# The first feed-forward's preparation moved into the attention ahead of it

## The chip, the cores and the metric

The kernel runs on one core of one Trainium2 chip. The time is device microseconds of one execution. The engines of a core are TensorE (matrix products and transposes through the array, into PSUM), VectorE, ScalarE, GpSimd, and SyncE, which here only issues loads. They run side by side and wait for each other through semaphores.

## The reference

A decoder block with gated cross-attention, four levels deep, over x of 4 batches of 1024 rows of 256. Every level adds a gated attention and a gated feed-forward:

```
x = x + tanh(g_xattn[0]) * attention_0(layernorm(x), ctx)
x = x + tanh(g_ffn[0])   * ffn_0(layernorm(x))
...                                    # three more levels
```

Attention 0 is a two-way cross-attention between x and 77 context rows with a sigmoid gate. Feed-forward 0 is a "bit linear" layer, a depthwise convolution over three neighbouring rows, SiLU, and a second bit linear layer:

```
def act_quant(x):                      # per row
    scale = 127.0 / clip(max(abs(x), axis=-1), 1e-05)
    return clip(round(x * scale), -128, 127) / scale
def weight_quant(w):                   # per matrix
    scale = 1.0 / clip(mean(abs(w)), 1e-05)
    return clip(round(w * scale), -1, 1) / scale
h = act_quant(x) @ weight_quant(w1).T  # 256 -> 1024
h = silu(depthwise_conv1d(h, conv_w, conv_b))
y = act_quant(h) @ weight_quant(w2).T  # 1024 -> 256
```

The mean of all of |w1| and of all of |w2| must be known before a weight can be rounded, and the maximum of a row before the row can be.

## The kernel before

All of x stays in SBUF, as 32 tiles of 128 rows by 256 (`sh.x`). The program is a row of eight stages, one function each. A stage opens a scope of its own for its tiles and semaphores; at its end all engines meet at a barrier and the semaphores are cleared. So nothing of a stage runs beside the stage before it.

**Stage 1, `stage_l0_xattn`** (attention 0). SyncE's queue loads the context, the weights and x batch by batch; ScalarE's queue loads biases, small weights and, last, the rows and the bands. The loop `for b in range(B)` runs over the 4 batches and is skewed: `out`, `gate` and `update` of batch b-1, in four quarters, stand between the steps of batch b. In order of time, for one batch, the names are these.

- VectorE `norm` makes the normalised rows. TensorE `front` transposes them (L915), ScalarE `turned` copies them (L679), and TensorE makes the scores in both directions (L878).
- VectorE `scores` (L758 to L769) takes maxima, ScalarE `exps` (L684, L689) the exponentials, VectorE `sums` (L776 to L779) the sums.
- TensorE transposes (L978), ScalarE copies them out (L706, `p2t`), and TensorE mixes the rows into the context (L989, into bank `ub`, "the mixing"). VectorE `mixed` (L783) scales the outcome.
- TensorE `out` (L967, L968), ScalarE `gate` (L697), VectorE `update` (L799 to L803, then the statistics of two tiles, L209), once for each quarter.

VectorE's order in batch b is `scores(b)`, `update(b-1, 0)`, `sums(b)`, `mixed(b)`, in batch 1 a norm chain over 16 tiles, `update(b-1, 1)`, `norm`, `update(b-1, 2)`, `norm`, `update(b-1, 3)`. The four updates of the last batch come behind the loop. `norm_range` is the norm chain: 19 small steps that turn statistics into a scale and a shift for each tile.

**Stage 2, `stage_l0_ffn`** (feed-forward 0). SyncE loads w1 and w2 (1 MB each) and two small arrays (`cw`, `cb`). Ahead of the loop over slots stands a chain: ScalarE sums |w1| and |w2| (L466, L468), TensorE adds the sums over the partitions (L371), VectorE makes the scales (L300 to L304). ScalarE loads the SiLU table (L472) and normalises tiles 0 to 7 (L479). VectorE takes their maxima (L283) and the scales, and rounds w1 in three passes (L307 to L309). ScalarE quantises the tiles (L486), VectorE takes the added constant off (L297), TensorE transposes them in four pairs through one bank (L380), and ScalarE copies each pair out (L493). Then comes ScalarE's scaling of w2 (L530), and the first up-projection (L390). A slot `g` is one batch and one of 8 blocks of 128 hidden rows: up-projection (L390), ScalarE's centre tap (L501), VectorE's two outer taps (L319, L321), ScalarE's SiLU (L507). The second layer follows 9 slots behind.

Of the kernel before, what the change touches and what calls it, by code (L numbers as in the profile page):

```python
# [16 lines left out]
P = 128  # L17
# [195 lines left out]
def stage_l0_ffn(nc, io, sh):  # L213
# [3 lines left out]
    s = scope(nc, "l0f")  # L217
    HID = 4 * D
# [7 lines left out]
    with s.ctx:  # L226
        norm_sems(s)
        w1, w2 = s.sb("w1", [P, DC, HID]), s.sb("w2", [P, M, D])
        w2q = s.sb("w2q", [P, M, D], BF16)
        wsum, wscale, wmean = s.sb("wsum", [P, 2]), s.sb("wscale", [P, 2]), s.sb("wmean", [P, 2])  # L230
        cw, cb = s.sb("cw", [P, M, 3]), s.sb("cb", [P, M])
        xn = s.sb("xn", [P, TB, D])
        am, sc, inv1 = (s.sb(n, [P, TB]) for n in ("am", "sc", "inv1"))
# [11 lines left out]
        for n in ["w_loaded", "small_loaded", "wsum_ready", "wtot_ps", "wscale_ready", "w1_ready", "w2_scaled", "w2_ready", "table_loaded",  # L245
                  "rstd_ready", "norm_ready", "step", "insc_ready", "q1_ready", "xd_ready", "xt_ps", "xt_ready", "h_ps", "a_ready",
                  "conv_ready", "z_ready", "am2_step", "sc2_ready", "inv2_ready", "zt_ps", "zq_ready", "back_ps", "q2_ready", "y_ps",
                  "x_ready", "stats_ready"]:
            s[n] = s.sem(n)
# [17 lines left out]
        with nc.Block() as block:  # L267
            @block.sync
            def _(sp):
                sp.dma_start(w1[:, :, :], io.L0_ffn_w1_T.rearrange("(c p) o -> p c o", p=P)).then_inc(s.w_loaded, 16)  # L270
                sp.dma_start(w2[:, :, :], io.L0_ffn_w2_T.rearrange("(c p) o -> p c o", p=P)).then_inc(s.w_loaded, 16)
# [4 lines left out]
            def _(dve):  # L276
                c = norm_vector(nc, dve, sh, s)
                dve.sem_inc(s.rstd_ready, 1)
                k = Chain(dve, s.step)

                def largest_input(b, j, n):
                    dve.wait_ge(s.norm_ready, b * TB + j + n)
                    k.link(nc.vector.tensor_reduce(am[:, j:j + n], xn[:, j:j + n, :], AX.X, ALU.max, apply_absolute_value=True))  # L283

                def input_scales(b):
                    k.link(nc.vector.tensor_scalar(am[:, :], am[:, :], 1e-5, None, ALU.max))
                    if b:
                        dve.wait_ge(s.xd_ready, b * TB)
# [3 lines left out]
                    dve.wait_ge(s.insc_ready, b + 1)  # L292
# [6 lines left out]
                dve.wait_ge(s.wtot_ps, 1)  # L299
                c.link(nc.vector.tensor_scalar(wmean[:, :], yb[:, 0:2], 1.0 / (HID * D), 1e-5, ALU.mult, ALU.max))  # L300
                nc.vector.reciprocal(wscale[:, :], wmean[:, :]).then_inc(s.wscale_ready, 1)
                dve.wait_ge(s.wscale_ready, 1)
                c.link(nc.vector.tensor_scalar(wmean[:, 0:1], wmean[:, 0:1], 1.0 / 127.0, None, ALU.mult))
                c.link(nc.vector.tensor_scalar(wmean[:, 1:2], wmean[:, 1:2], tg, None, ALU.mult))  # L304
# [64 lines left out]
            def _(pe):  # L369
                pe.wait_ge(s.wsum_ready, 2)  # L370
                nc.tensor.matmul(yb[:, 0:2], sh.ones[:, :], wsum[:, :], start=True, stop=True).then_inc(s.wtot_ps, 1)  # L371

# [50 lines left out]
                def down(t):  # L423
                    if t == 0:
                        pe.wait_ge(s.w2_ready, 1)
                        pe.wait_ge(s.wscale_ready, 1)
# [12 lines left out]
                pe.wait_ge(s.w1_ready, 1)  # L439
# [24 lines left out]
            def _(act):  # L464
                act.wait_ge(s.w_loaded, 32)
                nc.scalar.activation(z[:, 0:2, :], w1[:, :, :].rearrange("p m d -> p (m d)").rearrange("p (a b) -> p a b", a=2), ACT.Abs,  # L466
# [2639 lines left out]
```

## Time and profile before

| | us |
|---|---|
| median of three runs | 1948.39 (1948.32 to 1948.67) |
| the profiled execution's own time | 1948.08 |
| span of its profile | 1946.1 |
| TensorE / VectorE / ScalarE / GpSimd busy | 1656.8 / 1148.0 / 886.7 / 321.2 |

The profile is one execution. A row of a timeline gives the start, the busy time, the engine, the source line, the operation, the tile written and the tiles read, the shapes, and the number of instructions taken together; in square brackets stands the idle time of the engine ahead of it and what ended it. PE is TensorE, DVE VectorE, ACT ScalarE. Times are in us from the start of the span. The granted clock is TensorE's, as a share of full speed.

### The profile page before, as it was taken

The numbers are of one execution on the slowest core, as the hardware profiler recorded it, in microseconds if no ns is written. First come the engines' busy times: TensorE is split into PE (matmuls) and PEld (weight loads), VectorE is DVE, ScalarE is ACT, GpSimd is POOL, SyncE is SP. The second block draws the span as 40 slices with busy tenths as digits, with TensorE's granted clock in tenths as the row PEclk, the third lists the DMA queues.
The fourth block names the chain that finished last, engine by engine and source line by source line (L and its number), as shares of the span: only waits on it lengthen the run. The fifth ranks groups of instructions, "written<-read, shape, count | busy, mean of one in ns | idle before, by whom it ended". The sixth has DMA issues, their size and how long they took to land. (4 is left out here: it accounts for less than half of the span.)

```text
span 1946.1 us, 29978 instructions
## 1 busy us (share of the span) xinstructions
PE 1656.8 (85%) x10149; PEld 1254.6 (64%) x10149; DVE 1148.0 (59%) x2495; ACT 886.7 (46%) x1803; POOL 321.2 (17%) x359
## 2 busy tenths in 40 slices
PE   7895578896899997899997579999954999979998
PEld 5452245555677665588886269999944888854446
DVE  4765567676455556899887743322247889842115
ACT  2232567764443210365564345555544566533213
POOL 0000000000000001311100155555553111101110
PEclk9898799998899988999998779999977999979999
DMA  5001000002100000100001922222252000010002
GB/s 154 1 1 44 0 1 1 1 1 68 49 1 1 1 1 9 30 1 1 2 2 55 382 82 72 72 72 72 72 168 67 2 1 2 1 47 1 1 0 87
DMA packets 62845, 78.78 MB, mean 40 GB/s; under 512 B 13179, under 2 KB 52655, under 8 KB 62319
## 3 DMA queue, kind: packets, MB, share of 16 engines
q1 hardware_dynamic: 42967, 47.35, 7.4%
q0 software_dynamic: 7584, 20.72, 3.4%
q10 hardware_dynamic: 12152, 8.85, 1.5%
q8 instruction: 84, 1.38, 0.3%
q14 instruction: 58, 0.48, 0.1%
HBM read 58.16 MB, written 18.74 MB: 40 GB/s over the span
## 5 line engine op out<-in xcount | busy, mean ns | idle before, releaser
L2880 PEld LDWEIGHTS moe_bank<-moe_xt,moe_w1e 128*128 128x128 f32 x1264 | 155.0, 193 | 5.7 <-DVE moe_xt L2728 1.7
L2880 PE MATMUL moe_bank<-moe_xt,moe_w1e 128*128 128x128 f32 x1264 | 155.8, 277 | 1.1 <-DVE moe_xt L2728 1.1
L2890 PE MATMUL moe_bank<-moe_w,moe_xin 128*128 x632 | 149.3, 379 | 0.0
L2954 ACT ACTIVATE moe_xin<-moe_bank,moe_b 128x128 f32<-128x128 f32 x316 | 90.1, 368 | 125.8 <-PE moe_bank L2880 124.2
L390 PE MATMUL l0f_hb<-l0f_xt,l0f_w 128*128 128x512 f32 x256 | 126.0, 624 | 5.4 <-DVE l0f_a L321 3.8
L1092 POOL TENSOR_TENSOR all_x<-all_x,l1f_bias 128x256 f32 x32 | 23.1, 724 | 632.2 <-DVE l1f_xn L204 632.2
L2890 PEld LDWEIGHTS moe_bank<-moe_w,moe_xin 128*128 128x128 f32 x632 | 114.0, 190 | 12.3
L209 DVE BATCH_NORM_STATS2 all_stats<-all_x 128x6 f32<-128x256 f32 (+1 forms) x256 | 104.0, 422 | 8.4
L2737 DVE TENSOR_TENSOR moe_y<-moe_bank,moe_b2r 128x256 f32<-128x256 f32 x79 | 33.6, 425 | 119.0 <-PE moe_bank L2890 116.1
L2797 POOL DMA_INDIRECT moe_results<-moe_y,moe_row x79 | 78.0, 987 | 125.1 <-DVE moe_y L2737 121.1
L2728 DVE COPY moe_xt<-moe_bank 128x256 f32<-128x256 f32 x79 | 33.6, 425 | 106.2 <-PE moe_bank L2868 105.1
L1964 PE MATMUL l3f_bank<-l3f_xt,l3f_wx 128*128 128x512 f32 x192 | 88.1, 609 | 0.0
L2945 ACT ACTIVATE moe_w1e<-moe_w 128x1024 f32 x79 | 83.5, 1058 | 2.9 <-issue 1.9
L2404 PE MATMUL l3x_o_bank<-l3x_vrow,l3x_pt 128*128 128x136 f32 (+1 forms) x640 | 81.2, 282 | 0.0
L2792 POOL DMA_INDIRECT moe_xin<-moe_inputs,moe_token x79 | 76.8, 972 | 26.3 <-PE moe_bank L2868 21.0
L2404 PE MATMUL l2x_o_bank<-l2x_vrow,l2x_pt 128*128 128x136 f32 (+1 forms) x640 | 80.7, 281 | 0.0
L390 PEld LDWEIGHTS l0f_hb<-l0f_xt,l0f_w 128*128 128x128 f32 x256 | 47.0, 200 | 48.7 <-issue 47.8
L2404 PEld LDWEIGHTS l3x_o_bank<-l3x_vrow,l3x_pt 128*128 128x128 f32 (+1 forms) x640 | 77.1, 191 | 0.5
L319 DVE SCALAR_TENSOR_TENSOR l0f_a<-l0f_hb,l0f_cw,l0f_a 128x1023 f32<-128x1023 f32 x32 | 41.0, 1282 | 61.5 <-ACT l0f_a L501 61.5
L2404 PEld LDWEIGHTS l2x_o_bank<-l2x_vrow,l2x_pt 128*128 128x128 f32 (+1 forms) x640 | 76.4, 190 | 0.6
L2042 ACT ACTIVATE l3f_gate<-l3f_bank,l3f_cols 128x512 f32<-128x512 f32 x36 | 24.7, 687 | 105.4 <-PE l3f_bank L1972 105.4
L1886 DVE TENSOR_TENSOR l3f_prod<-l3f_gate,l3f_ct 128x512 f32<-128x512 f32 x12 | 8.3, 692 | 94.1 <-ACT l3f_gate L2042 94.1
(478 smaller groups left out, 3812.1 us busy)
## 6 DMA issues: line engine op xcount, KB each, us to landing
moe_w<-in_L_ffn_W SPq DMA_DIRECT2D x32, 512.0 KB, 10.3
moe_w<-moe_results SPq DMA_DIRECT2D x16, 512.0 KB, 8.8
all_x<-in_x SPq DMA_DIRECT2D x4, 1024.0 KB, 13.1
out_x<-all_x SPq DMA_DIRECT2D x8, 512.0 KB, 2.9
l0f_w<-in_L_ffn_w_T SPq DMA_DIRECT2D x2, 1024.0 KB, 6.4
moe_inputs<-moe_xin ACTq DMA_DIRECT2D x8, 256.0 KB, 7.3
moe_inputs<-moe_w1e ACTq DMA_DIRECT2D x8, 256.0 KB, 7.5
moe_b2r<-in_L_ffn_b SPq DMA_DIRECT2D x1, 2048.0 KB, 14.0
```

What stands on the lines that cost most here:

```text
L209: return nc.vector.bn_stats(sh.stats[:, ds(t * 6, 6)], x_tile(sh, t))
L319: k.link(nc.vector.scalar_tensor_tensor(a[:, u, 1:S], h[:, 0:S - 1], cw[:, m, 0:1], a[:, u, 1:S], ALU.mult, ALU.add))
L390: ins = nc.tensor.matmul(hb[g % 2][:, half * 512:(half + 1) * 512], w1[:, d, m * P:(m + 1) * P], xt[:, b % 2, d, half * 512:(half + 1) * 5 ...
L1964: ins = nc.tensor.matmul(bank[3 * m + k][:, :], wx[:, k, c, m * P:(m + 1) * P], xt[:, c, b * S + j * G:b * S + (j + 1) * G], start=(c == 0 ...
L2404: ins = nc.tensor.matmul(o_bank[:, m * VW:(m + 1) * VW], pt[0:rows(i), u, n, j * P:(j + 1) * P], vrow[0:rows(i), ds((t // TB) * (DC * NV * ...
L2728: nc.vector.tensor_copy(xt[:, u, :], bank[3 * u][:, 0:D]).then_inc(s.et_ready, 1)
L2792: nc.gpsimd.indirect_dma_start(out=gathered(t), out_offset=None, in_=xnd, in_offset=bass.IndirectOffsetOnAxis(ap=token[:, t:t + 1], axis=0 ...
L2797: nc.gpsimd.indirect_dma_start(out=ys, out_offset=bass.IndirectOffsetOnAxis(ap=row[:, t:t + 1], axis=0), in_=y[:, u, :], in_offset=None).t ...
L2880: ins = nc.tensor.matmul(out, w1e[:, at:at + P], xt[:, u, c * P:(c + 1) * P], start=(c == 0), stop=(c == DC - 1))
L2890: ins = nc.tensor.matmul(bank[4 + u][:, 0:D], ht[:, u, c * P:(c + 1) * P], w2[:, ds(e * (HC * D) + c * D, D)], start=(c == 0), stop=(c == ...
L2945: nc.scalar.activation(w1e[:, u * DC * HID:(u + 1) * DC * HID], w1[:, ds(e * (DC * HID), DC * HID)], ACT.Copy).then_inc(s.w1e_ready, 1)
L2954: ins = nc.scalar.activation(ht[:, u, m * P:(m + 1) * P], bank[1 + u][:, m * P:(m + 1) * P], ACT.Gelu, bias=b1[:, ds(e * HC + m, 1)])
```

## The change

The weights of feed-forward 0, their sums, scales and the rounding of w1, and the normalised rows of batch 0 with their maxima and scales are made in stage 1. Their tiles get a scope `sh.f0` around both stages. Both loads go to the end of SyncE's queue in stage 1. ScalarE's two Abs instructions stand at the end of the loop body of `b == 0`, behind `exps(1)`; they write to `w2q` in place of `z`. TensorE's sum over the partitions goes to the end of batch 1, ahead of `front(2)`, into bank `ub`. VectorE gets `weight_scales` (scales and the first pass over w1) at the end of batch 1, `round_weights` (the other two passes) at the end of batch 2, and in batch 3 `norm_range` over tiles 0 to 7 ahead of `update(2, 2)`, `next_inputs` (eight `normalise` steps, on VectorE now) ahead of `update(2, 3)`, and `next_scales` behind it. Stage 2 begins with the quantise steps. Its norm chain covers tiles 8 to 31 and stands behind the dequantise steps, and the SiLU table is loaded behind the four copies. The rounding of w2 stays where it was.

```diff
 # stage 2
-                sp.dma_start(w1[:, :, :], io.L0_ffn_w1_T.rearrange("(c p) o -> p c o", p=P)).then_inc(s.w_loaded, 16)
-                sp.dma_start(w2[:, :, :], io.L0_ffn_w2_T.rearrange("(c p) o -> p c o", p=P)).then_inc(s.w_loaded, 16)
...
-                c = norm_vector(nc, dve, sh, s)
-                dve.sem_inc(s.rstd_ready, 1)
+                c = Chain(dve, s.norm_step)
...
-                largest_input(0, 0, TB)
-                input_scales(0)
-                c.link(nc.vector.tensor_scalar(w1[:, :, :], w1[:, :, :], wscale[:, 0:1], MAGIC, ALU.mult, ALU.add))
-                c.link(nc.vector.tensor_scalar(w1[:, :, :], w1[:, :, :], MAGIC, 1.0, ALU.subtract, ALU.min))
-                nc.vector.tensor_scalar(w1[:, :, :], w1[:, :, :], -1.0, None, ALU.max).then_inc(s.w1_ready, 1)
                 for t in range(TB):
                     dequantise(t)
+                norm_range(nc, c, sh, TB, T)
+                dve.sem_inc(s.rstd_ready, 1)
...
                 for t in range(TB):
-                    norm(t)
-                for t in range(TB):
                     quantise_x(t)
                 for t in range(0, TB, 2):
                     copy_x(t)
-                act.wait_ge(s.wscale_ready, 1)
+                act.wait_ge(s.small_loaded, 32)
+                nc.scalar.activation(silu_in[:, :], cb[:, :], ACT.Silu).then_inc(s.table_loaded, 1)
+                act.wait_ge(s.table_loaded, 1)
 # stage 1: SyncE, ScalarE, VectorE, TensorE
+                sp.dma_start(f.w1[:, :, :], io.L0_ffn_w1_T.rearrange("(c p) o -> p c o", p=P)).then_inc(sh.f0_loaded, 16)
+                sp.dma_start(f.w2[:, :, :], io.L0_ffn_w2_T.rearrange("(c p) o -> p c o", p=P)).then_inc(sh.f0_loaded, 16)
...
                     if b + 1 < B:
                         turned(b + 1)
                         exps(b + 1)
+                    if b == 0:
+                        act.wait_ge(sh.f0_loaded, 32)
+                        nc.scalar.activation(f.w2q[:, :, :].rearrange("p m d -> p (m d)"), f.w1[:, :, :].rearrange("p m d -> p (m d)"), ACT.Abs,
+                                             accum_out=f.wsum[:, 0:1]).then_inc(sh.f0_wsum, 1)
+                        act.wait_ge(sh.f0_wsum, 1)
+                        nc.scalar.activation(f.w2q[:, :, :].rearrange("p m d -> p (m d)"), f.w2[:, :, :].rearrange("p m d -> p (m d)"), ACT.Abs,
+                                             accum_out=f.wsum[:, 1:2]).then_inc(sh.f0_wsum, 1)
...
                     if b + 1 < B:
                         norm(b + 1, 0, NP)
+                    else:
+                        dve.wait_ge(s.xn_ready, T)
+                        dve.wait_ge(s.stats_ready, 2 * TB)
+                        norm_range(nc, c, sh, 0, TB)
                     if b:
                         update(b - 1, 2)
                     if b + 1 < B:
                         norm(b + 1, NP, TB)
+                    else:
+                        next_inputs()
                     if b:
                         update(b - 1, 3)
+                        if b == 1:
+                            weight_scales()
+                        elif b == 2:
+                            round_weights()
+                        else:
+                            next_scales()
...
+                    if b == 1:
+                        pe.wait_ge(sh.f0_wsum, 2)
+                        pe.wait_ge(s.shared_set, 1)
+                        nc.tensor.matmul(ub[:, 0:2], sh.ones[:, :], f.wsum[:, :], start=True, stop=True).then_inc(sh.f0_wtot, 1)
                     if b + 1 < B:
                         front(b + 1)
```

## Rows read from the trace of the kernel before

**Rows 1.** The page: the span, and each engine's busy time.

```profile
span 1946.1 us, 29978 instructions
PE 1656.8 (85%) x10149; PEld 1254.6 (64%) x10149; DVE 1148.0 (59%) x2495; ACT 886.7 (46%) x1803; POOL 321.2 (17%) x359
```

**Rows 2.** Busy time by stretch: its length, engines (instructions), granted clock, DMA share, GB/s.

```profile
179.30:213.58 34.28, 5.01 (x18) 3.38 (x19) 13.01 (x39) 15.25 (x27) 0.00 (x0) 0.51 0.20 62
213.58:1946.10 1732.52, 1503.45 (x9507) 1161.37 (x9507) 1026.86 (x2176) 821.65 (x1672) 312.29 (x342) 0.94 0.12 40
```

**Rows 3.** Timeline of ScalarE, start of stage 2.

```profile
188.89 1.91 ACT L466 ACTIVATE l0f_z<-l0f_w 128x2048 f32<-128x2048 f32 x1 [13.05 <-DMA l0f_w<-in_L_ffn_w_T]
...
192.81 1.28 ACT L472 ACT_TABLE_LOAD   x1
...
194.34 4.04 ACT L479 ACTIVATE l0f_xn<-all_x,all_shift,all_rstd 128x256 f32<-128x256 f32 x8
201.60 3.30 ACT L486 ACTIVATE l0f_xn<-l0f_xn,l0f_sc 128x256 f32<-128x256 f32 x8 [3.22 <-DVE l0f_sc L291]
207.26 0.60 ACT L493 ACTIVATE l0f_xt<-l0f_back 128x512 f32<-128x512 f32 x1 [2.36 <-PE l0f_back L380]
...
219.18 1.20 ACT L501 ACTIVATE l0f_a<-l0f_hb,l0f_cb,l0f_cw 128x1024 f32<-128x1024 f32 x1 [2.87 <-PE l0f_hb L390]
```

**Rows 4.** Timeline of VectorE, start of stage 2.

```profile
180.67 0.21 DVE L168 TENSOR_TENSOR all_var<-all_stats 128x32 f32<-128x32 f32 x1 [1.38 <-PEq L107]
...
198.49 2.29 DVE L283 TENSOR_REDUCE l0f_am<-l0f_xn 128x8 f32<-128x2048 f32 x1 [4.22 <-ACT l0f_xn L479]
...
201.60 1.29 DVE L307 TENSOR_SCALAR l0f_w<-l0f_w,l0f_wscale 128x2048 f32<-128x2048 f32 x1
```

**Rows 5.** Timeline of TensorE, start of stage 2 (the second row holds two slots).

```profile
206.08 1.08 PE L380 MATMUL l0f_back<-all_ident,l0f_xn 128*128 128x128 f32 x4 [12.65 <-DVE l0f_xn L297]
...
213.58 8.99 PE L390 MATMUL l0f_hb<-l0f_xt,l0f_w 128*128 128x512 f32 x16 [0.84 <-ACT l0f_xt L493]
```

**Rows 6.** Busy time by stretch, early in stage 1 (columns as in rows 2).

```profile
28.00:30.00 2.00, 2.00 (x3) 0.50 (x2) 0.00 (x0) 0.00 (x0) 0.00 (x0) 0.50 0.03 8
```

**Rows 7.** Timeline of ScalarE, stage 1, batch 1.

```profile
75.52 0.72 ACT L706 ACTIVATE l0x_p2t<-l0x_sb 128x308 f32<-128x308 f32 x2
76.78 0.60 ACT L697 ACTIVATE l0x_th<-l0x_gb 128x512 f32<-128x512 f32 x1 [0.53 <-PE l0x_gb L968]
...
92.20 0.60 ACT L697 ACTIVATE l0x_th<-l0x_gb 128x512 f32<-128x512 f32 x1 [7.59 <-PE l0x_gb L968]
```

**Rows 8.** Timeline of TensorE, stage 1, batches 1 and 2.

```profile
76.58 3.62 PE L989 MATMUL l0x_ub<-l0x_xn,l0x_p2t 128*77 128x256 f32 x16
...
87.65 2.02 PE L967 MATMUL l0x_cb<-l0x_rhs,l0x_p1t 128*128 128x512 f32 x2 [3.58 <-DVE l0x_tmp L801]
...
120.29 1.10 PE L967 MATMUL l0x_cb<-l0x_rhs,l0x_p1t 128*128 128x512 f32 x2 [1.04 <-DVE l0x_tmp L801]
```

**Rows 9.** Timeline of VectorE, stage 1, from batch 0's norm chain to the last updates.

```profile
13.51 0.17 DVE L146 TENSOR_TENSOR all_var<-all_stats 128x8 f32<-128x8 f32 x1
...
17.10 2.67 DVE L204 TENSOR_SCALAR l0x_xn<-all_x,all_rstd,all_shift 128x256 f32<-128x256 f32 x8
...
81.57 0.48 DVE L783 TENSOR_SCALAR l0x_uu<-l0x_ub,l0x_inv 77x256 f32<-77x256 f32 x1
...
105.27 1.22 DVE L758 TENSOR_REDUCE l0x_m<-l0x_sb 77x1 f32<-77x1024 f32 x1 [3.17 <-PE l0x_sb L878]
...
136.22 1.22 DVE L758 TENSOR_REDUCE l0x_m<-l0x_sb 77x1 f32<-77x1024 f32 x1 [3.18 <-PE l0x_sb L878]
...
154.72 0.69 DVE L799 SCALAR_TENSOR_TENSOR l0x_tmp<-l0x_th,l0x_cb 128x512 f32<-128x512 f32 x1 [2.23 <-ACT l0x_th L697]
...
161.07 0.69 DVE L799 SCALAR_TENSOR_TENSOR l0x_tmp<-l0x_th,l0x_cb 128x512 f32<-128x512 f32 x1 [3.42 <-ACT l0x_th L697]
...
167.91 0.69 DVE L799 SCALAR_TENSOR_TENSOR l0x_tmp<-l0x_th,l0x_cb 128x512 f32<-128x512 f32 x1 [3.92 <-ACT l0x_th L697]
```

More of the change, by code:

```diff
@@ L483, in quantise_x @@
                     j = t % TB
-                    if j == 0:
-                        act.wait_ge(s.insc_ready, t // TB + 1)
+                    if j == 0 and t:
+                        act.wait_ge(s.insc_ready, t // TB)
                     nc.scalar.activation(xn[:, j, :], xn[:, j, :], ACT.Copy, bias=MAGIC, scale=sc[:, j:j + 1]).then_inc(s.q1_ready, 1)
@@ L568, in stage_l0_xattn @@
     s = scope(nc, "l0x")
+    f = sh.f0
+    HID = 4 * D
     SC = D ** -0.5
@@ L806, in update, with weight_scales, round_weights, next_inputs @@
                         tile_stats(nc, sh, t).then_inc(s.stats_ready, 1)
+                def weight_scales():
+                    dve.wait_ge(sh.f0_wtot, 1)
+                    c.link(nc.vector.tensor_scalar(f.wmean[:, :], ub[:, 0:2], 1.0 / (HID * D), 1e-5, ALU.mult, ALU.max))
+                    nc.vector.reciprocal(f.wscale[:, :], f.wmean[:, :]).then_inc(sh.f0_wscale, 1)
+                    dve.wait_ge(sh.f0_wscale, 1)
+                    nc.vector.tensor_scalar(f.wmean[:, 0:1], f.wmean[:, 0:1], 1.0 / 127.0, None, ALU.mult)
+                    c.link(nc.vector.tensor_scalar(f.wmean[:, 1:2], f.wmean[:, 1:2], sh.gates[:, 4:5], None, ALU.mult))
+                    c.link(nc.vector.tensor_scalar(f.w1[:, :, :], f.w1[:, :, :], f.wscale[:, 0:1], MAGIC, ALU.mult, ALU.add))
+                def round_weights():
+                    c.link(nc.vector.tensor_scalar(f.w1[:, :, :], f.w1[:, :, :], MAGIC, 1.0, ALU.subtract, ALU.min))
+                    nc.vector.tensor_scalar(f.w1[:, :, :], f.w1[:, :, :], -1.0, None, ALU.max)
+                def next_inputs():
+                    for j in range(TB):
+                        normalise(nc, sh, f.xn[:, j, :], j).then_inc(sh.f0_xn, 1)
+                def next_scales():
+                    dve.wait_ge(sh.f0_xn, TB)
+                    c.link(nc.vector.tensor_reduce(f.am[:, :], f.xn[:, :, :], AX.X, ALU.max, apply_absolute_value=True))
+                    c.link(nc.vector.tensor_scalar(f.am[:, :], f.am[:, :], 1e-5, None, ALU.max))
+                    nc.vector.tensor_scalar(f.inv1[:, :], f.am[:, :], f.wmean[:, 0:1], None, ALU.mult)
+                    c.link(nc.vector.reciprocal(f.sc[:, :], f.am[:, :]))
+                    nc.vector.tensor_scalar(f.sc[:, :], f.sc[:, :], 127.0, None, ALU.mult)
                 first(0)
@@ L985, in _ @@
                         pe.wait_ge(s.rows_ready, 2)
+                    if b == 2:
+                        pe.wait_ge(sh.f0_wscale, 1)
                     for t in range(TB):
@@ L3077, in program @@
         sh.ctx_t = sh.sb("ctx_t", [P, DC, B * SK])
-        stage_l0_xattn(nc, io, sh)
-        stage_l0_ffn(nc, io, sh)
+        for n in ("loaded", "wsum", "wtot", "wscale", "xn"):
+            sh[f"f0_{n}"] = sh.sem(f"f0_{n}")
+        sh.f0 = scope(nc, "f0")
+        with sh.f0.ctx:
+            M = 4 * D // P
+            sh.f0.w1, sh.f0.w2 = sh.f0.sb("w1", [P, DC, 4 * D]), sh.f0.sb("w2", [P, M, D])
+            sh.f0.w2q = sh.f0.sb("w2q", [P, M, D], BF16)
+            sh.f0.wsum, sh.f0.wscale, sh.f0.wmean = (sh.f0.sb(n, [P, 2]) for n in ("wsum", "wscale", "wmean"))
+            sh.f0.xn = sh.f0.sb("xn", [P, TB, D])
+            sh.f0.am, sh.f0.sc, sh.f0.inv1 = (sh.f0.sb(n, [P, TB]) for n in ("am", "sc", "inv1"))
+            stage_l0_xattn(nc, io, sh)
+            stage_l0_ffn(nc, io, sh)
         stage_l1_xattn(nc, io, sh)
```

42 lines of the change are left out of this document (10 added, 32 removed).

## Prediction

> **What bounds the kernel now.** The page comes first: TensorE is busy for 85% of the span [rows 1], so time is lost where it stands still. The busy time by stretch shows where: from the attention's last VectorE instruction (179.30) to the feed-forward's first up-projection (213.58) lie 34.28 us with only 5.01 us of TensorE [rows 2]. The timelines of the three engines in that stretch say what stands in series. The stage starts at 180.67, VectorE's first instruction after the barrier [rows 4]. ScalarE waits 13.05 us for the weights, sums both with Abs from 188.89 to 192.81, loads Silu's table, normalises eight tiles in 4.04 [rows 3]. VectorE reduces them in 2.29, computes scales, and rounds w1 behind that [rows 4]. ScalarE quantises eight tiles in 3.30 from 201.60 and makes the first of four copies at 207.26 [rows 3]. TensorE turns the tiles in four groups, slowly, and starts the up-projection at 213.58 [rows 5]. That is 213.58 - 180.67 = 32.9 us of preparation in one chain, and nothing else of the program runs beside it. Inside the attention the engines pass work in a ring with idle gaps; what is put into it costs only what the gap there doesn't hold.
>
> **What leaves the second stage.** The weight load, both Abs, the sum over partitions, the norms of tiles 0 to 7, their maxima and scales, and the rounding of w1 are done before the stage starts. What is left ahead of the up-projection: eight quantise steps (3.30), then the four copies with the transposes between them. From the first copy to the up-projection took 213.58 - 207.26 = 6.32 [rows 3, 5]. The first transposes and the first dequantise steps run beside the quantise steps, since each needs only its own tile. So the up-projection starts 3.30 + 6.32 = 9.6 us after the stage does, in place of 32.9: **-23.3 us**.
>
> Three things moved behind this must not surface. (1) Silu's table load and its first use, 194.34 - 192.81 = 1.53 us [rows 3], now stand behind the copies, ahead of w2's scaling and two norms. There ScalarE was idle for 2.87 us before the first centre step [rows 3], as that waits for the first slot of the up-projection. 1.53 fits in 2.87, 1.3 are left: 0. (2) VectorE's norm chain over 24 tiles goes behind the dequantise steps; by the 19 steps over 8 columns, 17.10 - 13.51 = 3.6 us [rows 9], it takes about 4, is done some 8 us into the stage, and is first needed by the norms behind w2's scaling, past 13 us: 0. (3) The two small loads go first on SP's queue instead of behind 2 MB. Before, they had landed by 192.81, 12.1 us into the stage with the weights ahead of them; now ScalarE wants them at 9.6. If they took as long as then, 2.5 us would be waited, of which 1.3 is covered: 0 to 1.2, taken as 0, because the 2 MB ahead of them are gone.
>
> **The loads inside the attention.** Two loads of 1 MB are queued on SP behind x; nothing on SP is behind them. Traffic has died down by 28 to 30 us (8 GB/s) [rows 6]. The second stage, with the same 2 MB and little else, waited 13.05 us [rows 3], so they are there by about 43 at the latest; ScalarE wants them at 75.5. They share the DMA engines with the attention's own last small loads on ScalarE's queue (bands, rows, the gate's weights), which TensorE and VectorE want from 35 us on. 0, with up to 1 us kept as a bound.
>
> The Trainium skill's page "DMA: Bandwidth & Descriptors", section "Queues, rings and completion order", says that each DMA engine takes turns between the queues packet by packet. It speaks against a free load: by it the small loads slow down beside w1 and w2. The trace has them late in the same company (x on SP's queue) and yet in time, so the sum stays; the rule is the reason for the bound and for a rival below.
>
> **The two Abs.** They stand on ScalarE behind the exponentials of batch 1 and ahead of the copies L706 at 75.52. Price: 192.81 - 188.89 = 3.92 [rows 3], plus some 0.2 for the new wait between them: 4.1. L706 moves to 79.6. The gate behind it had waited 0.53 for TensorE [rows 7], so it and VectorE's update move by 3.5 only. But TensorE's mixing (L989, 16 matmuls in 3.62) needs L706's copies [rows 8]. It can start near 80.05, after an idle time of some 3.3 us. At 87.65, after 3.58 us idle, a pair of matmuls took 2.02, at 120.29 after 1.04 us only 1.10 [rows 8]; and in the second stage the first slot took from 213.58 to about 219.1 and the second 3.5 [rows 3, 5]. So after such a gap a group pays about 2 us until the clock is up. The mixing then ends at 80.05 + 3.6 + 2.0 = 85.7, and VectorE's L783, at 81.57 before [rows 9], starts at 85.8: **+4.2**. Bounds: 3.5 (the clock stays up and VectorE's own chain decides) and 5.2 (all of the mixing at 2.02 / 1.10: 6.65 us, end 86.7). From L783 on VectorE works without a pause to its second update, so the delay is passed on whole.
>
> **The sum over partitions on TensorE.** Two passes with a 128x128 weight load, at 16 passes in 3.62 [rows 8] 0.23 each, about **+0.4**: it lies ahead of batch 2's transposes, for whose scores VectorE waited 3.17 at 105.27 [rows 9]. Nothing covers it.
>
> **VectorE's additions.** Weight scales: four tiny steps at 3.6 / 19 = 0.19 and a pass over w1 like L307 (1.29) [rows 4]: 2.1 into a gap of 3.17 [rows 9]: 0. Two more passes a batch later: 2.5 into 3.18 [rows 9]: 0. In batch 3 the norm chain of 3.6 stands ahead of the update at 154.72, whose gap was 2.23 [rows 9]: that update slips by 1.3. Then eight normalise steps, 2.67 [rows 9]. The update itself was 2.8 long, so they end at 154.72 + 1.3 + 2.8 + 2.7 = 161.5, where the next update began at 161.07: **+0.5**. TensorE's output block between the two is released by the first two steps of the slipped update, at about 157.5; it began there before too, as TensorE was in its band products until then. The maxima and scales, 2.29 [rows 4] and four small steps, 3.1 in all, go into 3.92 [rows 9]: 0. If the covers of these four were gone they would cost 2.1, 2.5, 6.3 and 3.1.
>
> **Sum.** The profiled execution took 1948.08, of which 1946.1 is its span [rows 1] and 2.0 lie around it; nothing of the change lies outside the span. 1948.08 - 23.3 + 4.2 + 0.4 + 0.5 = 1929.9. The median is 0.3 above that execution; 18.2 us less than the median is 1930.2. Forecast: **1930**, by itself 1928.5 to 1932. A measurement tells about 0.2%, 3.9 us, from no change.
>
> **Rivals.**
> *The clock stays up behind the mixing (0.14).* TensorE's gap ahead of L967 was 3.58 (84.07 to 87.65). The mixing now ends 5.5 us later (85.7 for 76.58 + 3.62), VectorE's release comes 4.2 later, so the gap shrinks to about 2.3, between the 3.58 that was followed by slow matmuls and the 1.04 that wasn't [rows 8]. If the clock stays up there the gate at 92.20, which waits for TensorE [rows 7], gains about 2 back: 1928.
> The Trainium skill's "TensorE: Matmul & The Clock Gate", "What's actually happening", says that how many matmuls run cold varies between runs of one kernel. By it the 2 us would come and go from run to run, 1928 or 1930; the three times of before lie within 0.35 us, which speaks for a fixed answer.
> *Uncovered remainders (0.18).* All of the mixing cold (+1.0), the small loads late (+1.2), the attention's loads slowed (+1) or ScalarE's remaining 1.3 used up: two of them give 1932 to 1933. For it: the remainders are thin. Against: each row by itself shows cover.
> *The change doesn't do what it says (0.02).* If the up-projection hangs on something not moved, only the overlap of Abs is gained: -3.9 + 5.1 makes 1949.6, no change. Against: the three timelines leave no other wait in the chain.
> *Slower (0.03).* The clock of TensorE in what follows. 1503.45 us of TensorE work come behind 213.58 at a granted clock of 0.94 [rows 2]; the 34 us of rest ahead of it shrink to 11. If less rest cost granted clock later, a loss of 18.2 / 1503 = 1.2% (0.94 to 0.929) eats the gain, and 1.5% gives 1953. For it: the clock does fall at times after 213.58. Against: the falls seen stand behind idle gaps [rows 5, 8], none behind long work.
> The forecast itself has 0.63. Faster by over 0.2% (below 1944.5): 0.63 + 0.14 + 0.18 = 0.95. Same: 0.02, slower: 0.03. Bounds of the sum: down to 1930 - 0.7 - 2 - 0.6 = 1926.7, up to 1930 + 1.0 + 1.2 + 1 + 1 = 1934. Range **1926.5 to 1934**.
>
> **What would show it.** Attention: L706 of batch 1 near 79.6 after two Abs; the mixing taking 5 to 6 us; the last VectorE instruction near 179.3 + 5.1 = 184.4. Second stage: up-projection about 9.6 us after VectorE's first instruction, near 195.4; ScalarE still idle ahead of the first centre step. VectorE's updates of batch 3: the third directly behind the norm chain, the fourth directly behind the normalise steps. From the up-projection to the end 1732.5 us as before [rows 2]. Wrong would be made by: a wait on the weights, a table load in the attention, a different clock behind the start of the up-projection.

## The result, and the profile after

The changed kernel took 1925.35 us (median of 4 executions, 1921.83 to 1926.29) where the kernel before took 1948.36 (1945.87 to 1948.67, 4) beside it: a ratio of 0.9881, interval 0.9864 to 0.9898. It is faster, as forecast. The size is past the forecast of 1930.0 and 1.2 us below the range's lower end of 1926.5. The profiled execution took 1925.29, with a span of 1923.1.

The page after, span and busy times, beside [rows 1]:

```profile
span 1923.1 us, 30011 instructions
PE 1655.1 (86%) x10149; PEld 1254.0 (65%) x10149; DVE 1152.3 (60%) x2522; ACT 883.4 (46%) x1795; POOL 322.6 (17%) x359
```

The work is the same, within 5 us on every engine, so the 23.0 us are time in which engines stood still. The busy time by stretch (columns as in [rows 2]) says where: first from the attention's last VectorE instruction to the first up-projection, then from there to the end, and then two stretches early in the attention.

```profile
179.16:189.94 10.78, 4.43 (x17) 2.86 (x17) 6.06 (x27) 5.61 (x13) 0.00 (x0) 0.56 0.06 2
189.94:1923.10 1733.16, 1503.40 (x9507) 1161.62 (x9507) 1026.09 (x2176) 824.17 (x1674) 313.67 (x342) 0.94 0.12 40
...
28.00:30.00 2.00, 2.00 (x4) 0.75 (x3) 0.00 (x0) 0.00 (x0) 0.00 (x0) 0.50 1.09 273
30.00:32.00 2.00, 2.00 (x8) 0.84 (x7) 0.15 (x1) 0.00 (x0) 0.00 (x0) 0.96 0.11 23
```

The reader sees three things. The preparation is 10.78 us where it was 34.28. From the up-projection on, the program takes as long as before (1733.16 for 1732.52) at the same granted clock of 0.94. And the two weight loads move 273 GB/s where the DMA engines had gone quiet at 8 [rows 6].

ScalarE, the attention's batch 1 and then the start of stage 2 (beside [rows 3, 7]):

```profile
73.02 1.89 ACT L710 ACTIVATE f_w2q<-f_w 128x2048 bf16<-128x2048 f32 x1
75.04 1.91 ACT L713 ACTIVATE f_w2q<-f_w 128x2048 bf16<-128x2048 f32 x1
76.95 0.72 ACT L680 ACTIVATE l0x_p2t<-l0x_sb 128x308 f32<-128x308 f32 x2
...
91.62 0.60 ACT L671 ACTIVATE l0x_th<-l0x_gb 128x512 f32<-128x512 f32 x1 [4.37 <-PE l0x_gb L986]
...
180.52 3.30 ACT L456 ACTIVATE f_xn<-f_xn,f_sc 128x256 f32<-128x256 f32 x8 [4.81 <-PEq L107]
...
189.90 1.28 ACT L498 ACT_TABLE_LOAD   x1
...
195.68 1.20 ACT L471 ACTIVATE l0f_a<-l0f_hb,l0f_cb,l0f_cw 128x1024 f32<-128x1024 f32 x1 [1.26 <-PE l0f_hb L372]
```

The Abs pair costs 76.95 - 73.02 = 3.93 and waits for no DMA. In stage 2 the quantise steps are the first thing ScalarE does, the table load stands behind the last copy, and 1.26 us of idle time are still left ahead of the first centre step.

TensorE (beside [rows 5, 8]):

```profile
26.45 5.36 PE L896 MATMUL l0x_sb<-l0x_xt,l0x_queries 128*77 128x512 f32 x8 [0.69 <-ACT l0x_xt L653]
...
77.50 5.34 PE L1009 MATMUL l0x_ub<-l0x_xn,l0x_p2t 128*77 128x256 f32 x16 [3.26 <-ACT l0x_p2t L680]
...
88.77 1.10 PE L985 MATMUL l0x_cb<-l0x_rhs,l0x_p1t 128*128 128x512 f32 x2 [2.06 <-DVE l0x_tmp L782]
...
97.76 0.28 PE L1037 MATMUL l0x_ub<-f_wsum,all_ones 128*128 128x2 f32 x2
```

The mixing waits 3.26 us and then takes 5.34 for 3.62. The pair behind it, which had come after 3.58 us of rest and taken 2.02, comes after 2.06 and takes 1.10: here the clock stayed up.

VectorE (beside [rows 9]):

```profile
82.95 0.48 DVE L764 TENSOR_SCALAR l0x_uu<-l0x_ub,l0x_inv 77x256 f32<-77x256 f32 x1 [0.63 <-PE l0x_ub L1009]
...
135.76 1.22 DVE L739 TENSOR_REDUCE l0x_m<-l0x_sb 77x1 f32<-77x1024 f32 x1 [0.78 <-PE l0x_sb L896]
...
155.53 0.69 DVE L780 SCALAR_TENSOR_TENSOR l0x_tmp<-l0x_th,l0x_cb 128x512 f32<-128x512 f32 x1
...
160.94 0.68 DVE L780 SCALAR_TENSOR_TENSOR l0x_tmp<-l0x_th,l0x_cb 128x512 f32<-128x512 f32 x1
```

The updates of batch 3 have no idle time ahead of them any more: they stand directly behind the norm chain and the normalise steps, as forecast.

Read alone, this pair of profiles says something odd. The attention ends at 179.16, no later than before (179.29), though 3.9 us of Abs stand in its ring. The wait that the prediction placed at VectorE's `mixed` is there: from the row maxima of batch 1, at 67.59, to 82.95 are 15.36 us, where 70.09 to 81.57 were 11.48. But batch 1 began 2.5 us earlier, ahead of every instruction of the change but two DMA issues. That is what the experiments had to settle.

### The profile page after: what moved, and what is told of

Its sections match the earlier page's. It is cut to its first block and busy times, and to the rows that moved or that the text cites. A ratio compares the mean times of both kernels' runs of the same rounds, so it can differ in the third digit from the quotient of the medians.

```text
span 1923.1 us, 30011 instructions
## 1 busy us (share of the span) xinstructions
PE 1655.1 (86%) x10149; PEld 1254.0 (65%) x10149; DVE 1152.3 (60%) x2522; ACT 883.4 (46%) x1795; POOL 322.6 (17%) x359
## 5 line engine op out<-in xcount | busy, mean ns | idle before, releaser
L372 PE MATMUL l0f_hb<-l0f_xt,f_w 128*128 128x512 f32 x256 | 126.1, 625 | 5.3 <-DVE l0f_a L306 3.9
L372 PEld LDWEIGHTS l0f_hb<-l0f_xt,f_w 128*128 128x128 f32 x256 | 47.0, 200 | 48.8 <-issue 46.7
## 6 DMA issues: line engine op xcount, KB each, us to landing
f_w<-in_L_ffn_w_T SPq DMA_DIRECT2D x2, 1024.0 KB, 13.6
```

Of the source, the lines that this page charges most:

```text
L372: ins = nc.tensor.matmul(hb[g % 2][:, half * 512:(half + 1) * 512], w1[:, d, m * P:(m + 1) * P], xt[:, b % 2, d, half * 512:(half + 1) * 5 ...
```

## The experiments

**Theory A** (the prediction's, with what the profile adds): the change gives 23.5 for the preparation, costs 3.9 at the mixing, and gains back up to 2 us because the gap ahead of the third output block of batch 0 shrinks. The rest is chance: in each execution TensorE's clock falls or doesn't behind the same gaps. **Theory B**: the early start of batch 1 belongs to the change, through the place of the tiles in SBUF or the loads in the attention. **Theory C**: something behind the up-projection got faster.

The first four kernels ran on one chip, with 25 executions of the kernel before beside them (median 1943.01, 1932.83 to 1949.95).

**Tiles held, nothing else**: the kernel before, with the new tiles reserved through the attention and not used.

```diff
+        f0 = scope(nc, "f0")
+        with f0.ctx:
+            f0.sb("w1", ...), f0.sb("w2", ...), f0.sb("w2q", ...), f0.sb("xn", ...)   # ... and the small ones
             stage_l0_xattn(nc, io, sh)
         stage_l0_ffn(nc, io, sh)
```

> The kernel before, with the new tiles (28 KB more per partition) held in SBUF during the attention and not used; same work. In the changed kernel the attention's first 75 us were 2.5 us shorter, which the prediction has no term for. Theory A (chance: where the first loads land and when TensorE's clock comes up differs from execution to execution): about 1948.4 as before, with the attention's exponentials of batch 1 anywhere between 72.7 and 75.2. Theory B (the place of the tiles in SBUF sets it): 1945.9, with the exponentials at 72.7.

Measured: 1937.01 us (1935.5 to 1945.19, 10 executions), ratio 0.9983, interval 0.9960 to 1.0006. Both expected totals stood on 1948.4, and the kernel before took 1943.01 beside this one. The interval includes 1, and it includes theory B's 2.5 us (0.13%) too, so the total decides nothing; the timelines have to.

**Loads only**: the kernel before, with the loads of w1 and w2 at the end of SyncE's queue in the attention, and everything else in stage 2.

```diff
 # stage 1, SyncE, behind the loads of x
+                sp.dma_start(sh.f0.w1[:, :, :], io.L0_ffn_w1_T...).then_inc(sh.f0_loaded, 16)
+                sp.dma_start(sh.f0.w2[:, :, :], io.L0_ffn_w2_T...).then_inc(sh.f0_loaded, 16)
 # stage 2, SyncE
-                sp.dma_start(w1[:, :, :], io.L0_ffn_w1_T...).then_inc(s.w_loaded, 16)
-                sp.dma_start(w2[:, :, :], io.L0_ffn_w2_T...).then_inc(s.w_loaded, 16)
```

> The kernel before, with the loads of w1 and w2 alone moved to the end of SyncE's queue in the attention; everything else stays in the second stage. The second stage's ScalarE starts Abs about 8.3 us earlier (188.89 - 180.6). Theory A (loads cost nothing in the attention and help nothing): 1948.4 - 8.3 = 1940.1. Theory C (the extra loads are what shortened the attention's start): 1937.6. Rival (they slow the attention's own loads): 1941 or more.

Measured: 1939.22 (1928.67 to 1942.07, 10), ratio 0.9978, interval 0.9953 to 1.0003. The stage itself did what was asked. Timeline of ScalarE:

```profile
177.97 1.91 ACT L464 ACTIVATE l0f_z<-f_w 128x2048 f32<-128x2048 f32 x1 [4.81 <-PEq L107]
```

The wait of 13.05 us for the weights is gone; the preparation is 26.05 us for 34.29, so 8.2 less (8.3 expected). The total can't tell it: 8.2 us are 0.42% and lie inside the interval, which the spread of the kernel before makes wide. That 1939.22 comes near the expected 1940.1 is luck: the expectation started from 1948.4, and before took 1943.01 beside it.

**Abs late**: the changed kernel with the Abs pair behind the copy of `ut` in batch 1, where ScalarE has a gap of 4.4 us.

```diff
 # stage 1, ScalarE, loop over b
                     act.wait_ge(s.ut_ps, b + 1)
                     nc.scalar.activation(ut[:, :, :], ...).then_inc(s.ut_ready, 1)
+                    if b == 1:
+                        act.wait_ge(sh.f0_loaded, 32)
+                        ...   (the two Abs)
                     if b:
                         gate(b - 1, 2)
...
-                    if b == 0:
-                        act.wait_ge(sh.f0_loaded, 32)
-                        ...   (the two Abs)
```

> The changed kernel, with the two Abs moved 9 us down ScalarE's queue, behind the copy of ut and ahead of the third gate of batch 1, where ScalarE idles. The mixing and all behind it come 3.9 us earlier. Theory (the clock follows the gap): TensorE's gap ahead of its third output block is again about 3.6 us, the block is slow again (2.0 for the first pair in place of 1.1) and 1.9 to 2.0 are given back: 1925.3 - 1.9 = 1923.4. Rival (the clock there has nothing to do with the gap): 1925.3 - 3.9 = 1921.4.

Measured: 1923.8 (1921.08 to 1928.2, 4), ratio 0.9896, interval 0.9857 to 0.9936. Timelines of ScalarE and TensorE:

```profile
82.54 1.93 ACT L693 ACTIVATE f_w2q<-f_w 128x2048 bf16<-128x2048 f32 x1
...
85.71 2.04 PE L985 MATMUL l0x_cb<-l0x_rhs,l0x_p1t 128*128 128x512 f32 x2 [3.57 <-DVE l0x_tmp L782]
```

The price of the mixing is gone (68.16 to 79.63 = 11.47, as before), but the gap ahead of the third output block is back at 3.57 and slow. From the maxima of batch 1 to the attention's end it took 110.54 where the first profile of the changed kernel has 111.57, and the two later ones (below) 112.85 and 112.08: 1.6 us less than their mean, and not 3.9. What Abs costs at one place is in part what VectorE's order costs at the next. The total of 1923.8 can't tell it from the changed kernel's 1923.6 to 1925.4.

**Idle matmuls in the gap**: the kernel before, with five matmuls on the identity into an unused bank ahead of the third output block, to keep the clock up.

```diff
+                    if b == 1:
+                        for _ in range(5):
+                            nc.tensor.matmul(sb2[:, 0, 0:P], sh.ident[:, :], sh.ident[:, :], start=True, stop=True)
                     if b:
                         out(b - 1, 2)
```

> The kernel before, with five matmuls on the identity (result not used) put into TensorE's gap of 3.58 us ahead of the third output block of batch 1, on a bank that is free. Theory (the clock falls because TensorE idles there): the gap shrinks to about 1.5, the first pair takes 1.1 in place of 2.0, the attention ends 2.0 earlier: 1946.4. Rival (the clock falls for another reason, or the matmuls delay the block): 1948.4 or more.

Measured: 1940.0 (lowest 1935.48, 10 executions; one of 5872.82 is an outlier), ratio 0.9992, interval 0.9963 to 1.0022. A miss, and the timeline of TensorE says why:

```profile
83.09 1.31 PE L1004 MATMUL l0x_sb<-all_ident 128*128 128x128 f32 x10
...
86.84 2.05 PE L967 MATMUL l0x_cb<-l0x_rhs,l0x_p1t 128*128 128x512 f32 x2 [2.44 <-DVE l0x_tmp L801]
```

They took 1.31 us and left 2.44 of rest (1.5 expected), and the pair was as slow as after 3.58. The expectation named 1946.4 or 1948.4; both stood on one execution of before, and the total shows no difference.

What these four say of theory B: the maxima of batch 1 start at 67.89 with the tiles held and at 67.81 with the loads moved, which alone would have fitted it; but also at 69.28 with the idle matmuls, whose edit has neither, and comes later. So an unchanged front varies by itself, and the two kernels had to be profiled again.

**Both kernels again, unchanged** (no edit): before twice more, after twice more.

> The kernel before, unchanged, for a second profile. Theory A (chance at the attention's start): the scores of batch 1 start anywhere from 67.6 to 70.1, and from there to the end of the attention it takes 109.2 us give or take 2 for the clock (before: 70.09 to 179.29; with the tiles only allocated: 67.89 to 176.90). Theory B (a property of the kernel): 70.1 again. Which of its two lengths the second level's attention takes (284.5 or 277.4 from its first load to the next stage's first VectorE step) changes as well between executions of one kernel, if theory A holds for the later stages too.

> The changed kernel, unchanged, for a second profile. The forecast's own terms are expected again: stage 2's preparation 10.8 us from the attention's end to the up-projection, the mixing about 5.3 and VectorE's step behind it 3.9 later. The clock ahead of the third output block of batch 1: theory A (chance of where the gap falls) allows 1.1 or 2.0 for the first pair, theory B (a gap of 2.06 never lowers it) only 1.1. From the scores of batch 1 to the end of the attention: 111.6 with the clock up as in the first profile, 113.5 with it down.

> The changed kernel unchanged, for more times and a third profile. If the change itself is worth the sum of its own terms as the two profiles gave them (-23.5 for the preparation, +3.9 for the Abs, +0.1 to 0.4 each for TensorE's sum and VectorE's additions, 0 to -2 for the clock ahead of the third block: -19 to -21) and the rest is chance of the clock, then the difference of the medians over many executions comes nearer to -20 than to -23. If there is a further systematic gain of 3 to 5, it stays at -23 or more, and the stretch behind the up-projection is shorter than before in most profiles. Attention's end, preparation of 10.8 and the two Abs as before.

> The kernel before unchanged, for a third profile beside the changed kernel's third. Scores of batch 1 between 67.6 and 70.3; the preparation 34.3; what follows the up-projection 1721 to 1734.

Measured: before 1948.85 (one execution; 7 more of the same kernel beside it 1944.47 to 1949.37) and 1942.14 (one; 12 beside it 1936.82 to 1948.73). After 1923.62 (1922.34 to 1924.96, 4), ratio 0.9876, interval 0.9860 to 0.9893, and 1923.63 (1916.24 to 1927.06, 6), ratio 0.9878, interval 0.9855 to 0.9900.

Read from the timelines of these ten profiles (us; "uu" is VectorE's L783 or L764 of batch 1, the fourth column the first instruction of the third update, the last one the rest of the program):

| kernel | first scores took | maxima of batch 1 | uu | third update | attention ends | to the up-projection | from there |
|---|---|---|---|---|---|---|---|
| before | 6.43 | 70.09 | 81.57 | 92.83 | 179.29 | 34.29 | 1732.5 |
| before, 2nd | 6.61 | 69.15 | 80.62 | 92.79 | 179.24 | 34.31 | 1733.4 |
| before, 3rd | 5.04 | 68.54 | 80.01 | 92.22 | 177.34 | 34.29 | 1728.6 |
| after | 5.36 | 67.59 | 82.95 | 92.25 | 179.16 | 10.78 | 1733.2 |
| after, 2nd | 6.27 | 70.26 | 85.61 | 96.48 | 183.11 | 10.79 | 1728.6 |
| after, 3rd | 6.29 | 69.36 | 84.72 | 95.59 | 181.44 | 10.80 | 1732.9 |
| tiles held | 5.36 | 67.89 | 79.36 | 90.49 | 176.90 | 34.40 | 1722.3 |
| loads only | 5.05 | 67.81 | 79.28 | 91.48 | 176.61 | 26.05 | 1734.2 |
| Abs late | 6.61 | 68.16 | 79.63 | 91.79 | 178.70 | 10.79 | 1732.6 |
| idle matmuls in the gap | 5.29 | 69.28 | 80.75 | 91.74 | 178.07 | 34.37 | 1721.1 |

The maxima of batch 1 start anywhere from 68.54 to 70.09 in one kernel and from 67.59 to 70.26 in the other. So theory B falls as the reason of the 2.5 us: the 2nd and 3rd profile of after have no such early start, and 183.11 and 181.44 for the attention's end. A small part of it isn't excluded: over all profiles of this document the maxima of batch 1 start at 68.50 on the mean of eight with the loads in the attention (without the one with idle matmuls ahead of them), and at 68.99 on the mean of five without. Theory C falls too: the last column of after has the values of before, and its spread of 13 us follows no edit.

The same instruction in the 2nd and 3rd profile of after, timeline of TensorE:

```profile
80.16 5.34 PE L1009 MATMUL l0x_ub<-l0x_xn,l0x_p2t 128*77 128x256 f32 x16 [3.25 <-ACT l0x_p2t L680]
...
91.42 2.04 PE L985 MATMUL l0x_cb<-l0x_rhs,l0x_p1t 128*128 128x512 f32 x2 [2.05 <-DVE l0x_tmp L782]
```

```profile
90.53 2.04 PE L985 MATMUL l0x_cb<-l0x_rhs,l0x_p1t 128*128 128x512 f32 x2 [2.04 <-DVE l0x_tmp L782]
```

The same program, the same gap (2.06, 2.05, 2.04): once the clock stayed, twice it fell. The mixing is alike in all three (5.34).

**Weights only**: the changed kernel with the norms, maxima and scales of tiles 0 to 7 back in stage 2.

```diff
 # stage 2, ScalarE (VectorE's norm chain, maxima and scales likewise)
+                for t in range(TB):
+                    norm(t)
                 for t in range(TB):
                     quantise_x(t)
 # stage 1, VectorE
-                        norm_range(nc, c, sh, 0, TB)
...
-                        next_inputs()
...
-                            next_scales()
```

> The changed kernel with only the weights' part in the attention; the norms of tiles 0 to 7, their maxima and scales are back in stage 2. Stage 2's chain becomes: norm chain 3.9, eight norms 4.1, maxima 2.4, scales 0.8, quantise steps 3.3, copies 6.3 and 0.2 between: 21.0, with 1.4 at the barrier 22.4 from the attention's end to the up-projection, in place of 10.8. The attention ends 0.3 earlier. Total 11.3 more than the changed kernel: 1936. Rival (the rows' part is hidden behind something else in stage 2): nearer to 1925.

Measured: 1928.73 (1922.54 to 1941.02, 5), ratio 0.9914, interval 0.9884 to 0.9943; the profiled execution was the one of 1941.02. Timelines of ScalarE and TensorE:

```profile
187.72 4.07 ACT L452 ACTIVATE f_xn<-all_x,all_shift,all_rstd 128x256 f32<-128x256 f32 x8 [8.97 <-DVEq L274]
...
77.85 6.65 PE L1006 MATMUL l0x_ub<-l0x_xn,l0x_p2t 128*77 128x256 f32 x16 [3.26 <-ACT l0x_p2t L685]
```

The preparation took 22.16 us (22.4 expected), so of the 23.5 gained the weights' part is worth 12.1 and the rows' part 11.4. The total is a miss: 1936 was expected, 11.3 more than the changed kernel, and the median is 5.1 more than the 1923.63 beside it. The five executions lie 18.5 us apart, so the split rests on the timelines, and the total neither confirms nor refutes it. The mixing took 6.65 here, after the same 3.26 us of rest: all of it slow, the prediction's upper bound for it.

**Late order**: Abs late, and in batch 1 VectorE's norm chain over 16 tiles behind `update(b - 1, 1)` instead of ahead of it, so that the third output block is released earlier.

```diff
                     mixed(b)
+                    if b:
+                        update(b - 1, 1)
                     if b == 1:
                         dve.wait_ge(s.first_stats, T)
                         norm_range(nc, c, sh, 2 * TB, T)
-                    if b:
-                        update(b - 1, 1)
```

> The changed kernel with the Abs in ScalarE's idle time (as in the third experiment) and, in batch 1, VectorE's norm chain of 16 tiles behind its second update instead of ahead of it. That chain made TensorE's gap of 3.6: with it gone the output block follows the transposes at once, the clock can't fall there, and VectorE reaches its third update some 4.5 us earlier than in the third experiment (4 from the chain's move out of the path at most, 2 from the clock, less what VectorE then has to do itself). Theory: scores of batch 1 to the end of the attention 106 to 107 us. Rival (VectorE is the bound there, not TensorE's gap): 108 to 110.

Measured: 1916.94 (1913.24 to 1920.68, 4), ratio 0.9850, interval 0.9834 to 0.9867, beside 1923.62 for the changed kernel on the same chip. Timeline of TensorE:

```profile
84.33 1.10 PE L985 MATMUL l0x_cb<-l0x_rhs,l0x_p1t 128*128 128x512 f32 x2 [1.04 <-DVE l0x_tmp L782]
```

The gap is 1.04 and the clock stays up. From the maxima of batch 1 to the attention's end are 105.88 us (106 to 107 expected), 5.7 to 7.0 less than in the three profiles of the changed kernel. How much of this is the order and how much the clock isn't told apart.

**Idle matmuls over the barrier**: the changed kernel with 14 idle matmuls behind the attention's last output block and 4 at the start of stage 2.

```diff
                 for q in range(NP):
                     out(B - 1, q)
+                for _ in range(14):
+                    nc.tensor.matmul(ub[:, 448:512], sh.ident[:, :], sh.ident[:, 0:64], start=True, stop=True)
 # stage 2
+                for _ in range(4):
+                    nc.tensor.matmul(yb[:, 256:384], sh.ident[:, :], sh.ident[:, :], start=True, stop=True)
                 for t in range(0, TB, 2):
                     turn_x(t, 0)
```

> The changed kernel with idle matmuls on the identity on TensorE between the attention's last block and the barrier (14) and at the start of stage 2 (4); results not used. Theory (the 10.8 us of what is left of the preparation hold cold transposes, and a cold first slot behind them, only because TensorE rested): the transposes take 0.63 in place of 1.11 for four, the first slot about 3.7 in place of 5.5, and the first centre step comes 3 us earlier. Rival (they delay the first transposes): up to 1 us later.

Measured: 1923.31 (1918.49 to 1926.52, 4), ratio 0.9877, interval 0.9855 to 0.9898. A miss. Timeline of TensorE:

```profile
180.54 2.05 PE L418 MATMUL l0f_yb<-all_ident 128*128 128x128 f32 x8 [2.40 <-PEq L107]
...
185.77 0.66 PE L362 MATMUL l0f_back<-all_ident,f_xn 128*128 128x128 f32 x4 [0.75 <-ACT l0f_xt L465]
187.17 1.11 PE L362 MATMUL l0f_back<-all_ident,f_xn 128*128 128x128 f32 x4 [0.75 <-ACT l0f_xt L465]
189.03 9.58 PE L372 MATMUL l0f_hb<-l0f_xt,f_w 128*128 128x512 f32 x16 [0.75 <-ACT l0f_xt L465]
```

The clock was down behind the 2.40 us at the barrier anyhow, as the idle matmuls' own 2.05 shows. Then it came up: two of the four groups of transposes took 0.66 and not 1.09 to 1.11, as expected for all. By the last group it was down again, behind rests of 0.75 only. The up-projection starts 0.9 us earlier, but the first centre step only 0.46 (195.22 for 195.68), since the first slots are slow (9.58 for 9.14).

**Late order with a warm front**: late order, and eight idle matmuls on TensorE ahead of the third pair of transposes of batch 0, which waits for normalised rows.

```diff
                         pe.wait_ge(s.xn_ready, b * TB + 2 * q + 2)
+                        if b == 0 and q == 2:
+                            pe.wait_ge(s.fold_ready, 2 * DC)
+                            for _ in range(8):
+                                nc.tensor.matmul(sb2[:, 0, 0:P], sh.ident[:, :], sh.ident[:, :], start=True, stop=True)
```

> The kernel of the seventh experiment (Abs late, norm chain behind the second update) with eight idle matmuls on the identity in TensorE's gap of 2.44 ahead of its third transposes of batch 0, on a free bank. Theory (the first scores take 5.1 to 6.6 in place of 3.7 because the clock falls in that gap): they take 3.7, the scores of batch 1 start 1.4 to 2.9 us earlier than without, between 65.5 and 67.5, and the total is 1.5 to 3 under the seventh's 1916.9. Rival (the fall isn't caused by that gap, or what is left of it is enough): the scores take 5 to 6.6 as ever.

Measured: 1915.45 (1910.61 to 1918.54, 5), ratio 0.9842, interval 0.9818 to 0.9866. That is the lowest median here, but 1.5 us to late order's 1916.94, measured on another chip, are inside the spread of both. Timeline of TensorE:

```profile
26.88 3.66 PE L896 MATMUL l0x_sb<-l0x_xt,l0x_queries 128*77 128x512 f32 x8 [0.69 <-ACT l0x_xt L653]
```

The first scores took 3.66 us, where the 13 profiles without those matmuls have 5.0 to 6.6, and the maxima of batch 1 start at 66.03, earlier than in any other profile.

## Why the prediction was right and wrong

**The preparation, -23.3: right.** 34.29 became 10.78 to 10.80 in all three profiles, -23.5. All three covers held. The table load and its use left 1.26 us ahead of the first centre step (1.3 forecast). VectorE's second norm chain made nothing wait. `cw` and `cb`, first in the queue, had landed 2.1 us after their issue. The weights-only run splits the gain: 12.1 and 11.4.

**The loads in the attention, 0: right.** w1 and w2 took 13.6 us to land, and from 30 us on the traffic is down to 23 GB/s, 40 us before Abs wants them. The rule of the Trainium skill weighed in the prediction ("DMA: Bandwidth & Descriptors", "Queues, rings and completion order") describes what happened: the small loads on ScalarE's queue took longer beside them (`wvg` 5.8 us to 8.0, `wv_o` 6.3 to 8.9, the rows 3.6 and 4.4 to 5.9 and 6.5). None of them was waited for.

**Abs and the mixing, +4.2: right in place, and in size within 0.3.** Abs took 3.93, the mixing 5.34, and `uu` came 3.88 us later behind the maxima than before, in three profiles of three (15.36, 15.35, 15.36 for 11.48, 11.47, 11.47). The upper bound of 5.2 was met once, in the weights-only run (16.67).

**TensorE's sum, +0.4, and VectorE's additions, +0.5: together half of that.** The two passes took 0.28 us. In batch 3, from the maxima to the attention's end, the three profiles of after have 43.40, 43.12 and 42.33 us, those of before 43.07, 43.06 and 41.37. From the third update of batch 1 to the attention's end, which holds both terms, the means are 86.46 and 86.01: +0.45.

**A term that the sum put at nothing: the block behind the shorter gap, -1.5 on the mean.** The prediction had the mechanism as its first rival, with a chance of 0.14: the mixing ends later, VectorE's release hardly later, so TensorE rests for about 2.3 us and not 3.58. It was 2.06. It took the gain as all (2 us, if the clock stays up) or nothing. From `uu` to the third update the three profiles of before have 11.26, 12.17 and 12.21, those of after 9.30, 10.87 and 10.87: 11.88 and 10.35 on the mean. Two more kernels run the changed code up to here, idle matmuls over the barrier and weights only:

```profile
88.76 1.10 PE L987 MATMUL l0x_cb<-l0x_rhs,l0x_p1t 128*128 128x512 f32 x2 [2.05 <-DVE l0x_tmp L784]
```

```profile
90.42 1.72 PE L982 MATMUL l0x_cb<-l0x_rhs,l0x_p1t 128*128 128x512 f32 x2 [2.05 <-DVE l0x_tmp L787]
```

They have 9.30 and 10.99, so the five have 10.27 on the mean. Tiles held and loads only, which run the code of before up to here, have 11.13 and 12.20, and these five 11.79: again 1.5. Of this, 0.26 has nothing to do with the clock: the block starts 5.8 us behind `uu` and not 6.1 in every profile, since VectorE's first norm step there takes 0.17 us and not 0.43 or 0.44. The rest is how long the block stays slow. Behind 3.58 us it was slow at its start five times of five; behind 2.05 it was fast twice of five, and that pays 1.6 to 1.7. That the shorter gap is the cause agrees with this, but so few executions don't prove it.

**The step that failed** is the bound on the clock. The sum put the clock ahead of the third output block at nothing, and the lower end allowed 2 us for it, 0.7 for Abs and 0.6 besides, in the whole program. The reason given is that the three times of before "lie within 0.35 us, which speaks for a fixed answer". The runs showed no fixed answer: the same program runs from 1916.24 to 1927.06 after the change, and from 1932.83 to 1949.95 before it, and what lies behind the up-projection alone differs by 13 us between profiles. Three times that agree to 0.35 us were a chance, and could not exclude this. They were also high: the sum starts from 1948.08, and the 25 executions of before on the three occasions when after ran beside it have a mean of 1946.1, which is 2.0 less. The Trainium skill's "TensorE: Matmul & The Clock Gate", "What's actually happening", says that how many matmuls run cold varies between runs of one kernel; the trace agrees, with 1.10 and 2.04 us for one pair after one gap. The prediction read that rule, applied it to one gap of the changed kernel, and not to the time of before, against which every sum is made.

**The account of the 23.0 us** between the first two profiles: attention -0.13, preparation -23.51, the rest +0.64. The attention's -0.13 is the early start of batch 1, -2.50, then +3.88 to `uu`, -1.96 to the third update, and +0.45 from there. By the change itself, with means in place of this one execution, it is -23.5 + 3.9 + 0.5 - 1.5 = -20.6, or 1927.5 from before's profiled time. That lies inside the range and 2.4 below the forecast's 1929.9: 0.2 from the preparation, 0.3 from Abs, 0.4 from the two small terms, 1.5 from the missing one. Between -20.6 and -23.0 lie, in this one pair of profiles, the 2.5 us by which the first profile of after began batch 1 earlier, which no edit explains and which the other two don't have, and two that nearly cancel: 0.4 to 0.5 more gained up to the third update than on the mean, and 0.6 lost behind the up-projection.

**What stays open.** All 14 executions of after have a mean of 1923.6. The 25 of before on the same three occasions have 1946.1, a difference of 22.5 (95%: 1.9 either way). With the other 25 of before, all 50 have 1943.9, and it is 20.4 (2.0 either way). The -20.6 of the timelines lies inside the second interval and at the edge of the first. So whether the change is worth 20.5 or 22.5 us isn't settled. The profiles give no sign of a further gain behind the up-projection: from there on the eight with the weights' preparation in the attention have 1731.1 us on the mean (1725.2 to 1734.8), the other six 1728.7 (1721.1 to 1734.2). A part of up to 2 us would be hidden in that spread. Which gaps leave the clock up in a given execution, and why, no run here shows.

## What to carry to other kernels

Work in front of a stage that waits for weights belongs into the stage ahead, and its gain can be read off the timelines to a few tenths; its price is set by the gap into which it is put, so look for one that the ring doesn't wait behind (Abs late and late order together gave 6.7 us more, another 0.35% of the kernel). A price or a gain that hangs on TensorE's clock behind a gap has a mean and a spread, not one value: profile the unchanged kernel three times before a range is set around a sum against one execution. Ahead of the third output block a gap of 1.04 us left the clock up in both profiles that have it, one of 2.04 to 2.06 twice in five, and those of 2.44, 3.57 and 3.58 were followed by slow matmuls each time.

## What the runs showed of the hardware

- One gap, two clocks: 2.06 us of rest were followed by a pair of matmuls of 1.10 us, 2.05 and 2.04 by pairs of 2.04, in three executions of the same program. In two kernels with the same code up to there, 2.05 us of rest were followed by 1.10 and by 1.72.
- The spread of a whole program: the kernel before took 1932.83 to 1949.95 us in 25 executions on one chip, 0.9%. The largest single piece found is the second level's attention. From the issue of its first load of small weights to VectorE's first instruction of the next stage it took 269.1 us in two profiles (tiles held, idle matmuls in the gap) and 274.4 to 277.3 in the twelve others, before and after alike, with the same code.
- Eight idle matmuls in a gap that TensorE has anyhow were followed by first scores of 3.66 us and not 5.0 to 6.6, in one profile against 13; behind five of them and 2.44 us of rest the next pair still took 2.05.
- A SiLU table load of 1.28 us behind the last copy: the next instruction of ScalarE starts 1.30 us after the load does.
